# Normalised rows split into two halves by GpSimd and transposed by the DMA engines, with the Q and K projections two and three steps later

## The reference

```python
x = x + 0.5 * ffn(layernorm(x), k0, k1, k2, s0, s1, s2)
x = x + attn(layernorm(x), Wq, bq, Wk, bk, Wv, bv, gamma, beta)
x = x + 0.5 * ffn(layernorm(x), k0, k1, k2, s0, s1, s2)

def ffn(x, ...):                       # weights are +1 or -1 by the booleans k0, k1, k2
    h = concatenate([x, -x], axis=-1)  # 256
    h = relu(s0 * (h @ w(k0))) * 2     # 512
    h = relu(s1 * (h @ w(k1))) * 2     # 512
    return s2 * (h @ w(k2))            # 128

def attn(x, ...):                      # 16 heads of 8, sequences of 256
    Q, K, V = x @ Wq.T + bq, x @ Wk.T + bk, x @ Wv.T + bv
    ctx = softmax(Q K^T / sqrt(8)) V   # per head
    return layernorm(ctx + x) * gamma + beta
```

## Time and profile before

| | before |
|---|---|
| median of three runs | 745.43 us |
| the profiled execution, its time | 745.53 us |
| the profiled execution, its span | 743.7 us |
| PE busy | 695.9 us (94%) |
| DVE busy | 649.1 us (87%) |
| ACT busy | 510.4 us (69%) |
| POOL busy | 365.9 us (49%) |
| share of the span on the chain that ended last | PE 70%, DVE 20%, ACT 3%, POOL 2%, DMA 1% |

### The profile page before, as it was taken

The page is one execution under the profiler, slowest core; times in us unless marked ns, Lnnn a source line. Parts: engine busy times, 40 slices in busy tenths (PEclk is TensorE's granted clock), DMA queues, the critical chain, the costliest instruction groups (busy, mean ns, idle before and its releaser), DMA issues.

```text
span 743.7 us, 18698 instructions
## 1 busy us (share of the span) xinstructions
PE 695.9 (94%) x7347; PEld 336.0 (45%) x7347; DVE 649.1 (87%) x1270; ACT 510.4 (69%) x745; POOL 365.9 (49%) x650
## 2 busy tenths in 40 slices
PE   7878999999999999999999999999999998787887
PEld 3434344544444454444444444444445444342346
DVE  6687898989999899999989898999989898887766
ACT  3426777777777777777787777767777776766644
POOL 6532455574454647454463746445465745254330
PEclk9999999999999999999999999999999999999999
DMA  3101010201102020201102020110201001010000
GB/s 82 57 15 52 16 53 2 65 17 45 37 3 66 17 66 16 67 17 29 39 16 66 16 66 17 44 38 2 67 17 65 17 33 36 30 38 2 11 7 30
DMA packets 29527, 25.65 MB, mean 34 GB/s; under 512 B 4353, under 2 KB 29441, under 8 KB 29441
## 3 DMA queue, kind: packets, MB, share of 16 engines
q1 hardware_dynamic: 27824, 23.74, 10.0%
q10 hardware_dynamic: 1616, 0.72, 0.3%
HBM read 5.05 MB, written 4.19 MB: 12 GB/s over the span
## 4 chain that ended last, share of the span: by engine, by line
PE 70%; DVE 20%; issue 4%; ACT 3%; POOL 2%; DMA 1%; SPq 0%; DVEq 0%; POOLq 0%
PE ps_c L876 15%; PE ps_z L702 13%; PE ps_z L703 11%; DVE row_max L1507 9%; PE ps_s L823 9%; DVE ffn_lo L1382 6%; PE ps_z L692 3%; PE ps_z L693 3%; PE ps_z L684 2%; PE ps_m L808 2%; PE ps_m L797 2%; ACT ffn_hi L1117 2%; PE ps_c L797 2%; PE ps_z L713 2%; DVE k_lo L1498 1%
## 5 line engine op out<-in xcount | busy, mean ns | idle before, releaser
L1507 DVE TENSOR_REDUCE row_max<-ps_s 128x4 f32<-128x1024 f32 x256 | 312.3, 1220 | 31.0 <-PE ps_s L823 29.3
L1156 ACT ACTIVATE probs<-ps_t,score_scale 128x1024 f32<-128x1024 f32 x252 | 280.2, 1112 | 62.2 <-PE ps_t L836 59.6
L1117 ACT ACTIVATE ffn_hi<-ps_z 128x512 f16<-128x512 f32 x261 | 149.8, 595 | 80.1 <-PE ps_z L703 63.2
L702 PE MATMUL ps_z<-ffn_hi,w 128*128 128x512 f16 x464 | 177.1, 382 | 0.8
L703 PE MATMUL ps_z<-ffn_lo,w 128*128 128x512 f16 x464 | 175.9, 379 | 0.0
L1382 DVE SCALAR_TENSOR_TENSOR ffn_lo<-ps_z,ffn_hi 128x512 f16<-128x512 f32 x232 | 154.3, 684 | 20.3 <-ACT ffn_hi L1117 17.4
L876 PE MATMUL ps_c<-probs,v_cols 128*32 128x256 f32 x2048 | 131.9, 386 | 1.3 <-ACT probs L1156 0.7
L823 PE MATMUL ps_s<-k_rows,q_rows 32*128 32x256 f16 x1024 | 100.2, 273 | 14.8 <-DVE row_max L1507 12.7
L836 PE MATMUL ps_t<-q_rows,k_rows 32*128 32x256 f16 x992 | 97.1, 273 | 0.0
L876 PEld LDWEIGHTS ps_c<-probs,v_cols 128*32 128x32 f32 x2048 | 57.0, 109 | 54.3 <-issue 26.6
L823 PEld LDWEIGHTS ps_s<-k_rows,q_rows 32*128 32x128 f16 x1024 | 29.0, 92 | 103.8 <-issue 50.4
(11 more groups left out here) (223 smaller groups left out, 1101.6 us busy)
## 6 DMA issues: line engine op xcount, KB each, us to landing
x<-L_attn_x SPq DMA_DIRECT2D x16, 256.0 KB, 2.7
q_rows<-q_hi SPq DMA_DIRECT2D x32, 128.0 KB, 2.5
k_rows<-k_hi SPq DMA_DIRECT2D x31, 128.0 KB, 2.1
y<-x SPq DMA_DIRECT2D x15, 256.0 KB, 2.2
q_rows<-no_max SPq DMA_DIRECT2D x16, 128.0 KB, 2.2
q_rows<-q_lo SPq DMA_DIRECT2D x16, 128.0 KB, 2.2
k_rows<-k_lo SPq DMA_DIRECT2D x15, 128.0 KB, 2.1
q_rows<-max_rows SPq DMA_DIRECT2D x64, 8.0 KB
```

What stands on the lines that cost most here:

```text
L702: pe.matmul(o[:], w, ffn_hi[:, 1 + k, :], start=(k == 0), stop=False)
L1117: a_.activation(ffn_hi[:, use, :], ps_z[use % 2][:], ACT.Relu if use else ACT.Copy, scale=1.0 if use else XN_SCALE).then_inc(z_hi, 1)
L1156: a_.activation(probs[n % PROBS][:, j:j + 2, :], o[:], ACT.Exp, scale=score_scale[:, 0:1]).then_inc(s_exp, 1)
L1507: v.tensor_reduce(row_max[hb % 2][:].rearrange("p (a l) e -> p l a e", a=2)[:, j:j + 2, :, g % 2], ps_s[:].rearrange("p l (a k) -> p l a k ...
```

## The change

The transposition leaves PE for 26 of the 29 feed-forwards of the loop and for the attention of all tiles but the first. In its place:

- POOL scales the reciprocal deviation (`ffn_rs_fit`, `att_rs_fit`), writes the upper half of the rows as 2-byte floats, writes the same product in float32, and subtracts the one from the other for the lower half: seven instructions in place of four. For the attention an eighth writes the float32 rows that `tail_base` adds.
- SP issues one DMA transposition of the eight 128x128 blocks, 256 KB, into `ffn_cols` or `att_cols`; PE's first product waits for its landing.
- ACT's and DVE's halves of piece 0 and of the attention's transposition are gone, and a feed-forward uses 9 in place of 10 turns of the two banks `ps_z`.
- Q goes from step 8 to 11, K from 11 to 13. The statistics of `ffn_a` are taken at steps 2 and 6 (mean and variance at 7) in place of 2 and 9 (10); the mean and variance of the next `ffn_b` go from step 27 to 26, those of the attention from 26 to 27. `tail_base` goes behind the first split of maxima.

```diff
-AT = {"LNT": 6, "Q": 8, "K": 11, "CT0": 14, "CT1": 22, "V": 25}
+AT = {"Q": 11, "K": 13, "CT0": 14, "CT1": 22, "V": 25}
-AT_STATS_A, AT_STATS_B, AT_STATS_PREP = ((2, 2, 9, 9), 10), ((24, 24, 25, 25), 27), ((18, 18, 20, 20), 26)
+AT_STATS_A, AT_STATS_B, AT_STATS_PREP = ((2, 2, 6, 6), 7), ((24, 24, 25, 25), 26), ((18, 18, 20, 20), 27)
...
+        FFNS_ON_PE = (0, second_ffn(T - 4), second_ffn(T - 3))
...
+            def turn_ffn(f):
+
+                sp.wait_ge(z_full, z_use(f - 1, 5))
+                sp.wait_ge(f_xn, f + 1)
+                sp.dma_start_transpose(ffn_cols[:], ffn_rows[:].rearrange("p i d -> p (i d)")).then_inc(s_cols, 16)
...
+            def turn_att(it):
+
+                sp.wait_ge(m_full, it.misc["Q"])
+                sp.wait_ge(a_xn, it.t + 2)
+                sp.dma_start_transpose(att_cols[:].rearrange("p (i n) -> p i n", n=P),
+                                       att_rows[:].rearrange("p i d -> p (i d)")).then_inc(s_att_cols, 16)
...
+            def ffn_rows_norm(f, src):
+
+                k = rs_steps(f)
+                pool.wait_ge(f_mv, f + 1)
+                g.tensor_tensor(ffn_ve[:], ffn_mv[:, :, 1], eps[:], ALU.add).then_inc(f_rs, 1)
+                g.tensor_tensor(ffn_xc[:], src[:], ffn_mv[:, :, 0:1].broadcast_to([P, TT, P]), ALU.subtract)
+                pool.wait_ge(f_rs, k + 1)
+                g.tensor_tensor(ffn_rs[:], ffn_ve[:], minus_half[:], ALU.pow).then_inc(f_rs, 1)
+                pool.wait_ge(f_rs, k + 2)
+                g.tensor_tensor(ffn_rs_fit[:], ffn_rs[:], xn_scale[:], ALU.mult).then_inc(f_rs, 1)
+                pool.wait_ge(f_rs, k + 3)
...
+                fit = ffn_rs_fit[:].unsqueeze(2).broadcast_to([P, TT, P])
+                g.tensor_tensor(ffn_rows[:, 0:TT, :], ffn_xc[:], fit, ALU.mult)
+                g.tensor_tensor(ffn_xn[:], ffn_xc[:], fit, ALU.mult).then_inc(f_rs, 1)
+                pool.wait_ge(f_rs, k + 4)
+                g.tensor_tensor(ffn_rows[:, TT:2 * TT, :], ffn_xn[:], ffn_rows[:, 0:TT, :], ALU.subtract).then_inc(f_xn, 1)
...
+                if by_dma(f) and m == 0:
+                    pe.wait_ge(s_cols, cols_landed(f))
```

More of the change, by code:

```diff
@@ L58 @@
 AT_MAX_EARLY = (10, 17, 25, 2)
-PREP_USES = ("LNT", "Q", "K", "V")
+PREP_USES = ("Q", "K", "V")
 Z_USES = 10
@@ L188, in macaron_layer @@
         solo_rs = sb("solo_rs", [P, TT])
+        ffn_rs_fit = sb("ffn_rs_fit", [P, TT])
+        ffn_rows = sb("ffn_rows", [P, 2 * TT, P], F16)
+        ffn_cols = sb("ffn_cols", [P, 2 * TT, P], F16)
         ffn_hi = sb("ffn_hi", [P, 9 + KC, TILE], F16)
@@ L296, in full, with by_dma, z_before, z_use @@
             return Iteration(t, r, ffn_a=second_ffn(t - 2), ffn_b=first_ffn(t + 2),
[L297 removed]
+                             next_b=first_ffn(t + 3) if t + 3 < T else None, misc_base=5 * t + 2)
         head = [Iteration(0, 0, prev=False, ffn_b=first_ffn(2), next_b=first_ffn(3), misc_base=4,
                           pace=PACE_ZERO),
[L301 removed]
+                Iteration(1, 1, ffn_b=first_ffn(3), next_b=first_ffn(4), misc_base=7)]
         LOOP_FROM, LOOP_TO = 2, TILES - 2
[L303 to L304 removed]
+        tail = [Iteration(T - 2, 0, ffn_a=second_ffn(T - 4), misc_base=5 * (T - 2) + 2, pace=PACE_ALONE),
+                Iteration(T - 1, 1, prep=False, ffn_a=second_ffn(T - 3), misc_base=5 * (T - 1) + 2,
                           pace=PACE_ALONE, own_contexts=True)]
[L306 removed]
+        L, L_PAR, L_USE = T - 1, (T - 1) % 2, 5 * (T - 1) + 4
         FFN_OF_L3 = second_ffn(T - 3)
         assert (LOOP_TO - LOOP_FROM) % 2 == 0 and LOOP_FROM % 2 == 0
+        FFNS_ON_PE = (0, second_ffn(T - 4), second_ffn(T - 3))
+        def by_dma(f):
+            return f not in FFNS_ON_PE
+        def z_before(f):
+            return sum(Z_USES - by_dma(n) for n in range(f))
+        def z_use(f, use):
+            return z_before(f) + use - by_dma(f)
+        def hi_made(f, use):
+            return z_use(f, use) - f + 1
+        def cols_landed(f):
+            return 16 * sum(by_dma(n) for n in range(f + 1))
+        def rs_steps(f):
+            return sum(4 if by_dma(n) else 2 for n in range(f))
+        def z_bank(f, use):
+            return ps_z[z_use(f, use) % 2]
         def run(eng, steps):
@@ L464, in steps @@
                     place_max(t - 1, 1 - par, 3)
+                if it.prep and it.prev:
+                    turn_att(it)
                 if it.cur and it.prev:
                     place_max(t, par, 0)
+                if it.first and it.prev:
+                    turn_ffn(it.next_b)
+                elif it.stats_a and by_dma(it.ffn_a):
+                    turn_ffn(it.ffn_a)
                 if not it.prev:
-                    sp.wait_ge(z_free, Z_USES)
+                    turn_ffn(it.ffn_b)
+                    sp.wait_ge(z_free, z_before(1))
                     sp.dma_start(x3[:].rearrange("p (b a) d -> p b a d", b=2),
@@ L489, in steps @@
                     place_max(t, par, 2)
+                if it.next_b is not None and (not it.first or not it.prev):
+                    turn_ffn(it.next_b)
                 if not it.prev:
-                    sp.wait_ge(z_free, Z_USES * (it.ffn_b + 1))
+                    sp.wait_ge(z_free, z_before(it.ffn_b + 1))
                     load_x(start_of(4))
             run(sp, steps)
-            sp.wait_ge(z_free, Z_USES * (FFN_OF_L3 + 1))
+            sp.wait_ge(z_free, z_before(FFN_OF_L3 + 1))
             store_x3(start_of(T - 3))
@@ L720, in ffn_piece @@
             def ffn_piece(f, s):
-                if s == 0:
+                if s == 0 and not by_dma(f):
                     ffn_transpose(f)
@@ L1114, in z_split @@
             def z_split(f, use):
-                act.wait_ge(z_full, Z_USES * f + use + 1)
-                a_.activation(ffn_hi[:, use, :], ps_z[use % 2][:], ACT.Relu if use else ACT.Copy,
-                              scale=1.0 if use else XN_SCALE).then_inc(z_hi, 1)
+                act.wait_ge(z_full, z_use(f, use) + 1)
+                if use:
+                    a_.activation(ffn_hi[:, use, :], z_bank(f, use)[:], ACT.Relu).then_inc(z_hi, 1)
+                else:
+                    a_.activation(ffn_cols[:, 0:TT, :], z_bank(f, 0)[:].rearrange("p (i n) -> p i n", i=TT), ACT.Copy,
+                                  scale=XN_SCALE).then_inc(z_hi, 1)
             def ffn_piece(f, s):
-                if s == 0:
+                if s == 0 and not by_dma(f):
                     z_split(f, 0)
@@ L1135, in att_split @@
                 act.wait_ge(m_full, use + 1)
-                a_.activation(att_hi[:], ps_m[:], ACT.Copy, scale=XN_SCALE).then_inc(m_hi, 1)
+                a_.activation(att_hi, ps_m[:], ACT.Copy, scale=XN_SCALE).then_inc(m_hi, 1)
             def qk_split(w, use, o=ps_m):
@@ L1559, in _ @@
                 if what == "LNT":
[L1560 removed]
+                    att_rest()
                 elif what == "Q":
```

139 lines of the change are left out of this document (78 added, 61 removed).

## The result

| | before | with the change |
|---|---|---|
| median | 744.84 us (744.24 to 748.40, four runs beside it) | 760.51 us (758.89 to 765.22, four runs) |
| ratio of the two | | 1.0211, 95% interval 1.0152 to 1.0269 |
| the profiled execution's span | 743.7 us | 757.1 us |

The change makes the kernel slower by 2.1%, from 1.5 to 2.7 by the interval; 755 us was forecast, with 739 to 775 as the range.

What follows compares the result with a forecast made beforehand. PE, 42.01 of 42.80 us busy per iteration, was taken to bound the loop; 11 x (43.40 - 42.74) = 7.3, plus 3.1 for the end, less 1 for the moved K, gave 9.4 on 745.5: 755 us, range 739 to 775.

Steps and rivals of the forecast that it cites:

- POOL's new price: POOL's norm takes 5.9 us to the feed-forward's rows, against 3.3, and 6.9 for the attention; busy near 480 us in all.
- The deadline of the first feed-forward: Rows ready at +0.93, PE's first product due at +2.20: PE waits L - 1.27 us per iteration, hidden by nothing.
- L: Time from a feed-forward's rows being ready until the transposed columns have landed and PE goes on; taken as 3.7 us.
- it fits: Rival, chance 0.22: L is 2.7 to 3.2 and the whole takes 743 to 749 us, about 745.5.
- The period is 42.74 - 1.77 + L - 1.27 = 39.70 + L: Loop period: the old one, less three transposition groups, plus PE's wait for the DMA; equal to before at L = 3.04.
- term 1.77: Three transposition groups of 0.59 us leave PE per loop iteration, each shortening the loop in full: 1.77 us.
- What ACT and DVE lose: ACT and DVE each lose a PSUM read per transposition group; counted as nothing because PE's bound hides it.
- PE bounds: PE is busy 42.01 of 42.80 us per iteration, so work leaving it shortens the loop and waits lengthen it one for one.
- What is late next: POOL's split for step 10 is met for L of 2.76 or more; Q has 1 us to spare, second feed-forward 0.4.
- the floor of 42.46: Below L of 2.76 POOL itself sets the loop's period at 42.46; an instant DMA would win only 0.28 us per iteration.
- The ends: First three iterations set equal; in the last full one POOL's longer attention norm costs 3.65 less one group, 3.1 us.
- the 1 us for the moved K: In the total, 1 us was taken off for idle time that the moved K fills.

## Why the prediction was right in its sign and near in its size

The periods make a ladder:

| kernel | period, us | step |
|---|---|---|
| before | 42.73 | |
| Q and K later | 43.08 | +0.35 |
| and the attention by DMA | 43.08 | 0.00 |
| and the second feed-forward by DMA | 42.29 | -0.79 |
| and the first one too (the change) | 43.54 | +1.25 |
| the same, its rows 5 us earlier | 42.48 | -1.06 |

- **POOL's new price** held: 5.8 us for 5.9, 475.7 us busy for about 480. The attention's took 6.76 (381.98 to 388.74) for 6.9.
- **The deadline of the first feed-forward** was the cause, as forecast. Its wait should have been L - 1.27; with the L found, 3.2, that is 1.9, and 1.75 was seen. L had been put at 3.7: 0.5 us too dear an estimate, inside its bounds of 2.7 and 4.8, and at the edge of what the text gave to "it fits", L of 2.7 to 3.2.
- **"The period is 42.74 - 1.77 + L - 1.27 = 39.70 + L"** is the step that failed, in its term 1.77. With L = 3.2 it gives 42.9; 43.54 was measured. The difference is 0.65 before the second weights and 0.36 before the scores, less 0.21 at L713 that went and 0.2 by which the DMA's wait fell below L - 1.27. I had written of the attention's group and of the moved Q and K that each counts in full or at nothing; the attention's 0.59 was in a shadow and was worth 0, and the move of Q and K cost 0.35. What ACT and DVE lose was counted as nothing; of DVE's halves one was worth 0.56 once Q and K had moved. The error of L and the error of the gain went opposite ways: 43.40 was forecast from two wrong terms, 0.14 off.
- **"PE's 94% busy" read as "PE bounds"** lies under that step. The earlier trace rows show 42.01 of 42.80 us busy, and three quarters of the two feed-forward groups, 0.88 us, won 0.16 when taken away. A nearly full engine hides how near the others are.
- **What is late next**: of the places named, none was met at an L of 3.2; with earlier rows the loop came to 42.48, close to the floor of 42.46 that the prediction gave for an instant DMA. But the prediction had POOL's split for step 10 set that floor. In the trace that split ends 0.6 us before PE needs it, and what holds PE back is DVE, 0.41 more, and the split for step 3, 0.3: the number was right by accident.
- **The ends**: 3.1 us were forecast for iteration 14. The waits came where they were said, for POOL and for DVE behind it:

```profile
644.25 0.36 PE L1005 MATMUL ps_m<-ident,max_parts 128*16 128x128 f16 x2 [2.57 <-POOL max_parts L671]
```

  From 619.63 to 639.20 before and 630.72 to 654.06 after, this stretch is 3.8 us longer, but 1.5 come back by the end, so 2.3 remain.
- **Unforeseen**: 2.8 us in one iteration, below. Per iteration 0.80 in place of 0.66, 1.7 us in all, and this one, less 0.5 at the two ends, explain why 13.4 us came for 9.4.
- **A slip in a rival**: "it fits" leaves out the 1 us for the moved K; with it the case runs from 744.5 to 749.4, not from 743. No run shows this 1 us; the move of Q and K by itself cost 0.35 an iteration.

## What to carry to other kernels

Before pricing work that leaves a busy engine, look at what stands behind each piece: if the next instruction's input is made by others in the meantime, the piece is free and its removal wins nothing. A transfer in place of computation is judged by when its source is ready and when its first reader stands, and this sum is made for each of its uses apart; here the same DMA won 0.79 us at one place, nothing at the second and lost 1.25 at the third, and without the third, with Q, K and the end moved, the kernel beat the one before by 0.9%. Not run was the second feed-forward alone by DMA, with the attention on PE and Q and K where they stood; by the ladder it might win as much, which is not shown. Moving a consumer later to hide a new latency also moves the work behind it into other work's way, which is best measured alone.
